# The final layer norm of a graph-transformer layer in groups of tiles, on one core

## The reference

```python
moe = w1 * e1 + w2 * e2                  # softmax weights of the two experts
z   = y + moe
mu  = mean(z);  var = var(z)             # over the 256 features
out = x + ((z - mu) / sqrt(var + 1e-5) * gamma + beta)
```

## Time and profile before

| what | value |
|---|---|
| median of 3 runs | 3555.98 us (3555.76 to 3556.52) |
| the profiled execution | 3530.59 us, its span 3528.9 us |
| first load of the final norm issued | 3388.67 us into the span |
| VectorE's last instruction begins | 3515.76 us |
| last store issued | 3519.39 us |
| PE, DVE, ACT, POOL busy over the span | 81%, 39%, 39%, 54% |

### The profile page before, as it was taken

The page is one execution under the profiler, slowest core; times in us unless marked ns, Lnnn a source line. Parts: engine busy times, 40 slices in busy tenths (PEclk is TensorE's granted clock), DMA queues, the critical chain, the costliest instruction groups (busy, mean ns, idle before and its releaser), DMA issues.

```text
span 3528.9 us, 48884 instructions
## 1 busy us (share of the span) xinstructions
PE 2849.1 (81%) x14412; PEld 2020.4 (57%) x14413; DVE 1378.7 (39%) x3854; ACT 1369.9 (39%) x2993; POOL 1914.3 (54%) x2019
## 2 busy tenths in 40 slices
PE   1899989999999998788888888888877648989930
PEld 0566656656656665555555555555556637878820
DVE  8455545555454453322222222222225541111157
ACT  4687777777777772000000000000004323333322
POOL 2656656566555564566666666666644551222245
PEclk9999999999999999898988999898888869999975
DMA  6344434434444445655555555555532344444444
GB/s 217 123 155 161 158 120 158 156 123 160 157 146 128 156 157 174 211 165 158 159 165 160 163 163 161 161 159 165 159 95 90 107 135 128 140 152 124 133 149 123
DMA packets 268417, 527.05 MB, mean 149 GB/s; under 512 B 58824, under 2 KB 155087, under 8 KB 268097
## 3 DMA queue, kind: packets, MB, share of 16 engines
q0 software_dynamic: 88848, 240.99, 23.0%
q1 hardware_dynamic: 148256, 252.66, 21.9%
q10 hardware_dynamic: 31120, 31.04, 2.7%
HBM read 394.15 MB, written 131.79 MB: 149 GB/s over the span
## 4 chain that ended last, share of the span: by engine, by line
PE 60%; issue 13%; DVE 8%; another core or an unknown queue 6%; ACT 4%; DMA 4%; SPq 3%; DVEq 1%; ACTq 0%; POOL 0%; POOLq 0%
PE bank L1033 28%; PE bank L1021 11%; PE sums L1047 6%; PE bank L1262 4%; DMA pa<-ys_d 3%; PE bank L1123 3%; PE bank L1061 2%; PE bank L1250 2%; PE bank L1072 1%; PE sums L1002 1%; ACT build L830 1%; PE bank L1131 1%; ACT build L832 1%; ACT pa L953 1%
## 5 line engine op out<-in xcount | busy, mean ns | idle before, releaser
L725 POOL DMA_INDIRECT pa<-xn_d,srcs x816 | 782.5, 959 | 513.6 <-PE sums L1047 278.9
L1033 PE MATMUL bank<-t1s,pa 128*128 128x256 f32 x2450 | 650.5, 412 | 96.3 <-issue 93.0
L725 POOL DMA_INDIRECT pa<-h_d,srcs x544 | 521.8, 959 | 305.5 <-issue 146.9
L1033 PEld LDWEIGHTS bank<-t1s,pa 128*128 128x128 f32 x2450 | 491.5, 207 | 243.4 <-issue 178.3
L1033 PE MATMUL bank<-t0s,pa 128*128 128x256 f32 x2450 | 573.3, 392 | 37.7 <-DVE pa L1438 36.7
L1021 PE MATMUL bank<-build 128*128 128x343 f32 x1500 | 489.7, 470 | 112.2 <-DVE build L1420 61.0
L1033 PEld LDWEIGHTS bank<-t0s,pa 128*128 128x128 f32 x2450 | 470.9, 195 | 140.9 <-issue 73.6
L1438 DVE TENSOR_TENSOR pa<-bank,pa 128x343 f32 x750 | 361.4, 511 | 385.0 <-ACT pa L837 172.9
L1021 PEld LDWEIGHTS bank<-build 128*128 128x128 f32 x1500 | 274.9, 193 | 303.2 <-issue 196.7
L832 ACT ACTIVATE build<-build,ones 128x343 f32<-128x343 f32 x750 | 436.3, 582 | 24.4
L830 ACT ACTIVATE build<-build,tabs 128x343 f32<-128x343 f32 x750 | 424.9, 567 | 34.6 <-issue 27.4
(11 more groups left out here) (257 smaller groups left out, 2739.5 us busy)
## 6 DMA issues: line engine op xcount, KB each, us to landing
slab_d<-pa SPq DMA_DIRECT2D x175, 448.0 KB
pa<-slab_d SPq DMA_DIRECT2D x175, 448.0 KB
pa<-in_w ACTq DMA_DIRECT2D x32, 512.0 KB
pa<-in_w SPq DMA_DIRECT2D x32, 512.0 KB, 3.6
pa<-ys_d SPq DMA_DIRECT2D x109, 130.0 KB
pa<-xn_d,srcs POOLq DMA_INDIRECT x816
pa<-eo_d SPq DMA_DIRECT2D x49, 256.0 KB, 3.2
pa<-h_d,srcs POOLq DMA_INDIRECT x544
```

What stands on the lines that cost most here:

```text
L725: pool.indirect_dma_start(gath2[b * QT + j], None, table, bass.IndirectOffsetOnAxis(ap=srcs[:, n:n + 1], axis=0)).then_inc(s_g[b], 16)
L1033: ins = pe.matmul(app[i % 2][:, 0:D], slab3[:, s, :], table[:, s * D:(s + 1) * D], start=s == 0, stop=s == T - 1)
```

## The change

The buffers of the final norm become 3 groups of 6 tiles with two tiles of room each (`a` and `b`), and the 49 tiles go in nine groups: 3, seven times 6, and 4 tiles. In each group VectorE does all first sums (`f_sums`), then reciprocal and bias of the group before in one operation each (`f_scales`), then all second sums, all bn_stats, all bn_aggr and one var + eps (`f_moments`). ScalarE does one root a group and then its norms. POOL ends tiles 0 to 41, VectorE ends tiles 42 to 48 (`f_ends`). SP now issues the stores too, in the order of the tiles; it waits until all stores of a group have landed and then issues the loads of the group three on. All of the stage is written out, without loops.

```diff
@@ class Links @@
-        self.eng.wait_ge(self.sem, self.at + (self.n - back))
+        self.eng.wait_ge(self.sem, self.n - back)
@@ buffers @@
-        FS = 8
-        cr = [pa[:, b * 4 * D:(b + 1) * 4 * D] for b in range(FS)]
+        FN, FB, FV = 6, 3, 7
+        FGR = [(0, 3)] + [(n, min(n + FN, T)) for n in range(3, T, FN)]
@@ SP @@
-            in_turns(sp, T, FS, f_load)
+            def f_load(g):
+                for u in range(*FGR[g]):
+                    sp.dma_start(fpair[g % FB][:, u - FGR[g][0]], rows(ekn, u)).then_inc(s_f_ld[g % FB], 16)
+            def f_store(g):
+                for u in range(*FGR[g]):
+                    if u < T - FV:
+                        sp.wait_ge(s_f_out, u + 1)
+                    else:
+                        sp.wait_ge(s_f_outv, u - (T - FV) + 1)
+                    sp.dma_start(rows(out, u), fy[g % FB][u - FGR[g][0]][0]).then_inc(s_f_st[g % FB], 16)
+            for g in range(FB):
+                f_load(g)
+            for g in range(len(FGR)):
+                f_store(g)
+                sp.wait_ge(s_f_st[g % FB], 16 * through(g))
+                if g + FB < len(FGR):
+                    f_load(g + FB)
@@ POOL @@
-            in_turns(pool, T, FS, c_tile)
+            for g, (first_u, end_u) in enumerate(FGR):
+                for u in range(first_u, min(end_u, T - FV)):
+                    a, b = fy[g % FB][u - first_u]
+                    pool.wait_ge(s_f_ln, u + 1)
+                    pool.tensor_tensor(b, b, gam, ALU.mult).then_inc(s_f_xb, 1)
+                    pool.wait_ge(s_f_xb, u + 1)
+                    pool.tensor_tensor(a, b, t0s[:, u * D:(u + 1) * D], ALU.add).then_inc(s_f_out, 1)
@@ ACT @@
-            in_turns(act, T, FS, f_root)
+            def f_root(g):
+                act.wait_ge(s_f_var, g + 1)
+                act.activation(fsd[:, FGR[g][0]:FGR[g][1]], fvar[:, FGR[g][0]:FGR[g][1]], ACT.Sqrt).then_inc(s_f_sd, 1)
+            def f_norm(g):
+                act.wait_ge(s_f_r, g + 1)
+                for u in range(*FGR[g]):
+                    a, b = fy[g % FB][u - FGR[g][0]]
+                    act.activation(b, a, ACT.Identity, bias=fnb[:, u:u + 1], scale=frs[:, u:u + 1]).then_inc(s_f_ln, 1)
+            for g in range(len(FGR)):
+                f_root(g)
+                f_norm(g)
@@ DVE @@
+            def f_sums(g):
+                dve.wait_ge(s_f_ld[g % FB], 16 * sum(FGR[n][1] - FGR[n][0] for n in range(g % FB, g + 1, FB)))
+                for u in range(*FGR[g]):
+                    a, b = fy[g % FB][u - FGR[g][0]]
+                    own.post(dve.scalar_tensor_tensor(out=a, in0=a, scalar=pw[0][:, u:u + 1], in1=y3[:, u, 0:D],
+                                                      op0=ALU.mult, op1=ALU.add))
+            def f_moments(g):
+                first_u, end_u = FGR[g]
+                n = end_u - first_u
+                for u in range(first_u, end_u):
+                    a, b = fy[g % FB][u - first_u]
+                    own.until(n - 1)
+                    own.post(dve.scalar_tensor_tensor(out=a, in0=b, scalar=pw[1][:, u:u + 1], in1=a,
+                                                      op0=ALU.mult, op1=ALU.add))
+                for u in range(first_u, end_u):
+                    own.until(n - 1)
+                    own.post(dve.bn_stats(fst6[:, u - first_u, :], fy[g % FB][u - first_u][0]))
+                for u in range(first_u, end_u):
+                    own.until(n - 1)
+                    own.post(dve.bn_aggr(fmva[:, u, :], fst6[:, u - first_u, :]))
+                own.until(0)
+                dve.tensor_scalar(fvar[:, first_u:end_u], fmva[:, first_u:end_u, 1], EPS, None, ALU.add
+                                  ).then_inc(s_f_var, 1)
+            def f_scales(g):
+                a = slice(*FGR[g])
+                dve.wait_ge(s_f_sd, g + 1)
+                link(dve.reciprocal(frs[:, a], fsd[:, a]))
+                dve.scalar_tensor_tensor(out=fnb[:, a], in0=fmva[:, a, 0], scalar=-1.0, in1=frs[:, a],
+                                         op0=ALU.mult, op1=ALU.mult).then_inc(s_f_r, 1)
+            def f_ends(g):
+                tiles = range(max(FGR[g][0], T - FV), FGR[g][1])
+                for u in tiles:
+                    b = fy[g % FB][u - FGR[g][0]][1]
+                    dve.wait_ge(s_f_ln, u + 1)
+                    own.post(dve.tensor_tensor(b, b, gam, ALU.mult))
+                for n, u in enumerate(tiles):
+                    a, b = fy[g % FB][u - FGR[g][0]]
+                    own.until(len(tiles) - 1 - n)
+                    dve.tensor_tensor(a, b, t0s[:, u * D:(u + 1) * D], ALU.add).then_inc(s_f_outv, 1)
+            for g in range(len(FGR)):
+                f_sums(g)
+                if g > 0:
+                    f_scales(g - 1)
+                f_moments(g)
+            f_ends(len(FGR) - 2)
+            f_scales(len(FGR) - 1)
+            f_ends(len(FGR) - 1)
```

More of the change, by code:

```diff
@@ L86, in __init__ @@
     def __init__(self, eng, sem):
-        self.eng, self.sem, self.at, self.n = eng, sem, 0, 0
+        self.eng, self.sem, self.n = eng, sem, 0
     def link(self, ins):
@@ L91, in link @@
         self.n += 1
-        self.eng.wait_ge(self.sem, self.at + self.n)
+        self.eng.wait_ge(self.sem, self.n)
     def post(self, ins):
@@ L122, in in_pairs @@
     tile(half * 2, 0, half, True)
[L125 to L133, removed]
 def wait_from(eng, sem, value):
@@ L327, in gps_layer @@
         eplc = [sb(f"eplc{b}", [P, 1], I32) for b in range(2)]
-        FS = 8
-        cr = [pa[:, b * 4 * D:(b + 1) * 4 * D] for b in range(FS)]
-        cy = [[cr[b][:, n * D:(n + 1) * D] for n in range(4)] for b in range(FS)]
-        crs = [build[:, 3200 + 4 * b:3204 + 4 * b] for b in range(FS)]
-        cmv = [build[:, 3240 + 2 * b:3242 + 2 * b] for b in range(FS)]
+        FN, FB, FV = 6, 3, 7
+        FGR = [(0, 3)] + [(n, min(n + FN, T)) for n in range(3, T, FN)]
+        fy = [[[pa[:, ((b * FN + q) * 2 + k) * D:((b * FN + q) * 2 + k + 1) * D] for k in range(2)] for q in range(FN)]
+              for b in range(FB)]
+        fpair = [pa[:, b * FN * 2 * D:(b + 1) * FN * 2 * D].rearrange("p (q k d) -> p q k d", k=2, d=D) for b in range(FB)]
+        fst6 = after[:, 0:6 * FN].rearrange("p (q s) -> p q s", s=6)
+        fmva = after[:, 64:64 + 2 * T].rearrange("p (q m) -> p q m", m=2)
+        fvar, fsd, frs, fnb = (after[:, 192 + 64 * k:192 + 64 * k + T] for k in range(4))
         nt_i = build[:, 3260:3276].bitcast(I32)
@@ L681, in _, with through @@
             ekn = eo_d.rearrange("(k n) d -> n k d", k=2)
[L683 to L686, removed]
-            in_turns(sp, T, FS, f_load)
-            for b in range(FS):
-                sp.wait_ge(s_f_st[b], 16 * len(range(b, T, FS)))
+            def through(g):
+                return sum(FGR[n][1] - FGR[n][0] for n in range(g % FB, g + 1, FB))
+            def f_load(g):
[15 more added lines that the diff above has]
+                    f_load(g + FB)
         @block.gpsimd
@@ L1760, in _ @@
             in_pairs(dve, half_of(dve), e_tile)
[L1763 to L1777, removed]
-                                                      op0=ALU.mult, op1=ALU.add))
[L1779 to L1788, removed]
```

46 lines of the change are left out of this document (2 added, 44 removed).

## The result

| | before | changed | ratio, 95% interval |
|---|---|---|---|
| median of the runs | 3556.25 us | 3523.81 us | 0.991 [0.9895, 0.9925] |
| the changed kernel again (e1), in another session | 3514.66 us | 3482.96 us | 0.9897 [0.9852, 0.9943] |
| profiled execution: first load of the final norm | 3388.67 | 3420.63 | |
| last store issued, after that load | 130.7 us | 104.7 us | |
| end of the span, after the last store's issue | 9.5 us | 3.3 us | |

One of the 19 executions of the kernel before in the second row took 11786 us, in the slow state, and the ratio leaves it out.

What follows compares the result with a forecast made beforehand. VectorE was taken to bound the final norm, 140 us of 3529. Last store at 3492.8 against 3519.39 gives 26.6, less 0.7 for late stores, 26 us; 3555.98 - 26 = 3530 us, range 3522 to 3541.

Steps and rivals of the forecast that it cites:

- What follows the last store is kept.: End of the kernel: the time behind the last store's issue was assumed unchanged by the change.
- The rest of the sum: Final norm up to the last store's issue: forecast at 3492.8 against 3519.39, 26.6 us earlier.
- 0.7 us for four late stores: End of the stage: four stores issued within 1.2 us land some 0.7 us later than one alone.
- The turn of 0.87 us: Final norm: two-input operations of VectorE and POOL exclude each other and take turns, a pair in about 0.87 us.
- The first rival: Second sums: POOL keeps the port at its seam, 1.54 us a sum, period 12.8, 3535 us; chance 0.20.
- The longer turn of 1.01: Port lock held for the whole instruction: 1.01 us a turn, period 12.7, 3535 us; held by the first rival.
- A full group of 12.0 us: Final norm: one full group of six tiles takes 12.0 us, 2.0 a tile.
- The buffer loop: Full groups: POOL's end, stores landing 3.0 us, six loads 6.5 us, then sums; two periods 24.0 us.
- The wait of 1.7 us a group: Full groups: loads in at 20.6, wanted at 18.9, so VectorE waits 1.7 us for them.
- The first group: Start of the final norm: three tiles, first load at 3388.67, in SBUF at 3392.5.
- The bn work: VectorE in each group: six bn_stats, six bn_aggr and the add of eps take 2.75 us, POOL running freely beside.
- Stores behind loads at no cost: SP's queue: a group's stores queue behind the loads of the group two on, costing nothing; uncovered, at most 6.5 us.

Runs made afterwards that it cites:

- e2: Changed kernel with POOL ending all 49 tiles, VectorE none: last store 109.0 us after the stage's first load, end 118.5 us, ratio to before 0.9948.
- e3: Changed kernel with VectorE ending the last ten tiles instead of seven: last store 105.2 us after the stage's first load, end 107.5 us.
- e4: Kernel before, tile by tile, without loops in the stage, VectorE ending the last seven tiles: stage end 131.0 us, ratio to before 0.9975.
- e7: Changed kernel with four buffers of five tiles instead of three of six: last store 103.4 us after the stage's first load, end 106.4 us.
- e6: Changed kernel with POOL's two operations on one column of each tile instead of 256: last store 85.8 us after the first load, end 88.0 us.
- e8: Changed kernel, POOL ending two tiles per group except the last, held until VectorE's bn work; VectorE ends the rest: stage end 99.8 us, ratio to before 0.9891.
- e11: e9 without POOL's wait for VectorE's bn work: last store 104.9 us after the stage's first load, end 107.2 us, 12.03 us a group.
- e9: e8 without VectorE's add of eps, which ScalarE's root takes as bias: last store 97.0 us, stage end 99.9 us, ratio to before 0.9881.
- e5: Changed kernel with VectorE ending all 49 tiles, POOL without work in the stage: last store 103.8 us, end 106.0 us, ratio to before 0.9902.

## Why the prediction was right, and where it wasn't

The result lies in the range, 1.8 us above its lower end, and the cause is the one named, but the gain was 32 us and not 26, and the difference is one term.

- *"What follows the last store is kept."* This step failed. The 9.5 us behind the last store belonged to POOL's drain, which counts from POOL's last instruction. The change moves that instruction 6 us ahead of the last store, and the end comes 3.3 us behind the store: 6.2 us that the sum left out. The rows were in the trace of before. e2, e3 and e4 show it from both sides.
- *The rest of the sum* was 26.6 us up to the last store's issue; measured 26.0 (130.7 - 104.7). The step of 0.7 us for four late stores was needless: the last store landed in 1.8 us.
- *The turn of 0.87 us* measured 0.86 (1.72 a tile), at both seams. The first rival, POOL keeping the port at its own seam, would have shown sums of 1.5 us; the longest of the 98 took 1.02. The longer turn of 1.01, by the reading that the lock is held for the whole instruction, isn't there either. There were fewer turns than forecast: of the 84 sums in full groups 39 took over 0.8 us and not two thirds, and POOL was idle 2.1 to 2.9 us in each of the four middle groups and not 1 to 2.
- *A full group of 12.0 us* measured 12.1 in the mean from reciprocal 2 to 6, 11.56 for the one forecast at 11.6, 11.02 for the one at 10.8. Reciprocal 8 was forecast 99.5 us after the first load and came at 100.0.
- *The buffer loop.* The wait of 1.7 us a group was 1.3 in the mean of four. Its parts were mis-sized against each other: stores landed in 1.8 us at the median instead of 3.0, six loads took 7.9 us instead of 6.5 (issued at 3455.14, first sum at 3463.07). From POOL's last operation of a group to the first sum on the new loads it came to 9.4 to 9.8 us against 3.0 + 6.5 = 9.5: the two errors offset each other, which was luck. The loop counts for less than the prediction says: with the waits gone (e7) only about 1 us comes back.
- *The first group* was expected 3.8 us after the first load and came 5.1 us after it, with twelve more loads issued behind its three; that these held it up was not tried. Reciprocal 0 was 0.6 us late by it, and the next period of 9.0 instead of 9.65 gave that back. *The bn work* took 2.57 us with the add of eps free (3437.09 to 3439.66) and up to 2.9 with it blocked, against 2.75; the prediction has no blocking of the add.
- *Stores behind loads at no cost:* true for this kernel, not for a faster one (e6).

Where the 32 us come from: 9.2 from giving VectorE the last seven tiles, shown in e4, with the 0.7 us of the loops in them; the other 23 from doing the tiles in groups. Taken in the other order, e2 has the groups at 21.7 (140.2 - 118.5), and the seven tiles bring 10.5 more.

The 23 us are hardly time that POOL had blocked. By the mean lengths against the free ones, VectorE lost about 25 us of the stage to POOL before (20 in the column operation, 5 in the sums) and about 24 after (21 in the sums, the rest in the adds of eps and one final multiply). This is an estimate from the groups by line. What became shorter is VectorE's time without POOL: the first tiles before came 1.85 us apart (3391.56 to 3395.27 is two of them), the free groups of e6 take 7.6 / 6 = 1.27 a tile. Over 49 tiles that is 28 us, from which the waits for loads and the later first group take some 8 back; the 20 that are left are near the 23. How much of it is small operations on one column and how much waits of VectorE for itself, no run separates.

The turns stay: the one full group without a wait for loads took 11.56 us against 7.6 in e6, the next four 10.9 in the mean with their waits of 1.3 taken out, so 3 to 4 us a group are turns and the blocked add of eps. e6, e8 and e11 price them.

## What to carry to other kernels

Where VectorE and POOL work on the same tiles, count what each operation of POOL takes from VectorE before counting what it takes off it: here 0.47 us of blocking for each that met a sum, against 0.34 us of work, so that POOL paid only while VectorE ran bn_stats and bn_aggr, and a semaphore that holds POOL back until then was worth 8 us (e9 against e11). And ask which engine works last: the end of a kernel has a tail of its own on each engine, and one with a long tail should have its last instruction early.

## What the runs showed of the hardware

- POOL's drain at the end took 9.3 us from the end of its last operation in every run, whatever stood ahead of it: tensor_tensor of 256 columns (10.08 to 10.22 us from its start), of one column (9.56 in e6), or an indirect DMA with an idle stage behind it (10.52 from 3410.7 in e5). VectorE's, ScalarE's and SP's were 0.01 to 2.6 us, work in flight included. In all 13 profiles the span ended 0.21 to 0.24 us behind the later of POOL's drain and SP's. What POOL does in it stays open.
- A tensor_scalar with one SBUF input on 5 or 6 columns waited for POOL (0.36 and 0.39 us in the mean, 0.72 in e8, 0.17 free), one on a single column before never did (0.15 in the mean of 49, with POOL inside an operation at the start of 35 of them). The Trainium skill (SBUF — State Buffer, "Who interferes with whom") says that tensor_scalar can enter a mode that uses the shared port pair too, and so contend, when its operands meet certain conditions; these rows agree, and show that a few columns are enough. The prediction gave the page's rule for one input without this exception, and so left out 0.2 to 0.3 us a group.
- An operation of POOL may begin up to about 0.15 us before the end of VectorE's without being held up, so the exclusion is a little shorter than the recorded durations: turns of 0.86 us where 0.29 + 0.72 would make 1.01.
- VectorE and POOL took turns wherever both had two-input operations waiting, but for one case: in e9 POOL's add was held for 3.24 us by eight tensor_tensor operations of VectorE in a row.
